# A recommendation tower on one core: ten of the first block's 32 table gathers replaced by comparisons and TensorE products, and the split of the second filter cut into pieces

## The reference, cut to what matters

```python
e = jnp.stack([tbl_f[ids[:, f]] for f in range(32)], axis=1)     # (512, 32, 32), all fp32
for W in (filter_0, filter_1):                                   # (1024, 128), (4096, 128)
    z = jnp.einsum('bhd,bmd->bhmd', e, prev)                     # prev: e, then the first layer
    cur = relu(jnp.einsum('bpd,pn->bnd', z.reshape(b, h * m, d), W)); prev = cur
h = concatenate([sum over d of both layers, dense_ctx], axis=1)  # (512, 272)
y = relu(relu(h @ W_top1 + b1) @ W_top2 + b2) @ W_top3
```

## Time and profile before

| | |
|---|---|
| median of 3 runs | 885.71 us (884.96 to 886.36) |
| profiled execution | 882.99 us |
| its span (first to last instruction) | 881.2 us |
| around the span | 1.8 us |
| PE matmul / DVE / ACT / POOL busy | 94% / 88% / 82% / 75% |

### The profile page before, as it was taken

The page is one execution under the profiler, slowest core; times in us unless marked ns, Lnnn a source line. Parts: engine busy times, 40 slices in busy tenths (PEclk is TensorE's granted clock), DMA queues, the critical chain, the costliest instruction groups (busy, mean ns, idle before and its releaser), DMA issues.

```text
span 881.2 us, 18094 instructions
## 1 busy us (share of the span) xinstructions
PE 832.6 (94%) x3608; PEld 669.4 (76%) x3608; DVE 771.7 (88%) x2425; ACT 724.7 (82%) x2425; POOL 662.0 (75%) x645
## 2 busy tenths in 40 slices
PE   0189999999999999999999999999999999999998
PEld 0068888888887788887888878888888888888875
DVE  4248999999998999998999999999999999999995
ACT  2248889988888899888888988888889988888883
POOL 7777898878887888868888878876677766666662
PEclk9999999999999999999999999999999999999999
DMA  7035776667667666666677666766776667657540
GB/s 197 12 88 129 176 170 148 134 127 172 153 152 168 156 151 142 127 158 154 155 174 166 145 135 130 169 145 151 171 168 141 133 135 158 153 138 171 96 93 5
DMA packets 78622, 124.42 MB, mean 141 GB/s; under 512 B 34177, under 2 KB 36993, under 8 KB 78594
## 3 DMA queue, kind: packets, MB, share of 16 engines
q0 software_dynamic: 22240, 68.17, 40.9%
q1 hardware_dynamic: 56354, 55.96, 21.0%
HBM read 54.99 MB, written 3.05 MB: 66 GB/s over the span
## 4 chain that ended last, share of the span: by engine, by line
PE 80%; POOL 9%; issue 5%; DVE 3%; DMA 2%; ACT 0%; POOLq 0%; DVEq 0%; ACTq 0%
PE bank L879 68%; PE bank L819 10%; POOL rows L349 4%; DVE acc L780 2%; POOL pair_low L384 2%; DMA parts<-parts 1%; POOL w_sb L368 1%; POOL rows_next L399 1%; PE bank L885 1%; POOL parts L361 1%; PE bank L911 1%; PE bank L850 1%; DVE acc L790 0%; POOL half L368 0%; DMA rows<-table_dram,ids_sb 0%
## 5 line engine op out<-in xcount | busy, mean ns | idle before, releaser
L560 ACT ACTIVATE parts<-bank,x 128x128 f32<-128x128 f32 x2048 | 588.0, 379 | 98.3 <-PE bank L879 87.2
L780 DVE SCALAR_TENSOR_TENSOR acc<-bank,x,acc 128x128 f32<-128x128 f32 x1792 | 484.2, 341 | 44.6 <-PE bank L879 44.6
L879 PE MATMUL bank<-w_high,cur_high 128*128 128x512 f32 x1024 | 402.3, 393 | 0.8 <-ACT cur_high L507 0.7
L879 PE MATMUL bank<-w_low,cur_high 128*128 128x512 f32 x1024 | 399.5, 390 | 0.0
L879 PE MATMUL bank<-w_high,cur_low 128*128 128x512 f32 x992 | 388.3, 391 | 0.0
L879 PEld LDWEIGHTS bank<-w_high,cur_high 128*128 128x128 f32 x1024 | 192.3, 188 | 48.2 <-DVE acc L780 6.4
L879 PEld LDWEIGHTS bank<-w_low,cur_high 128*128 128x128 f32 x1024 | 192.4, 188 | 40.0
L879 PEld LDWEIGHTS bank<-w_high,cur_low 128*128 128x128 f32 x992 | 186.2, 188 | 40.6
L384 POOL TENSOR_TENSOR pair_low<-pair,pair_high 128x512 fp32r<-128x512 f32 x124 | 158.8, 1300 | 22.0 <-ACT pair_high L496 19.2
L368 POOL TENSOR_TENSOR half<-parts 128x512 f32<-128x512 f32 x64 | 82.8, 1293 | 120.0 <-DMA parts<-parts 119.9
L399 POOL DMA_INDIRECT rows_next<-table_dram,ids_next x96 | 97.9, 1019 | 30.6 <-issue 30.3
(11 more groups left out here) (96 smaller groups left out, 557.9 us busy)
## 6 DMA issues: line engine op xcount, KB each, us to landing
parts<-parts POOLq DMA_DIRECT2D x126, 512.0 KB, 6.7
shifts<-x_scratch SPq DMA_DIRECT2D x155, 256.0 KB, 3.9
x<-x_scratch SPq DMA_DIRECT2D x31, 256.0 KB, 2.9
x_scratch<-turned SPq DMA_DIRECT2D x124, 24.0 KB
rows_next<-table_dram,ids_next POOLq DMA_INDIRECT x96, 5.0
wt<-w_top_dram SPq DMA_DIRECT2D x2, 512.0 KB, 9.1
rows<-table_dram,ids_sb POOLq DMA_INDIRECT x32, 2.4
w_sb<-w_ab_dram SPq DMA_DIRECT2D x1, 256.0 KB, 3.0
```

What stands on the lines that cost most here:

```text
L560: ins = nc.scalar.activation(parts[q][ab][:, at:at + N2], act_bank[ab][:, i * N2:(i + 1) * N2], ACT.Copy, scale=x0[u][:, h, 2 * q + ab:2 * ...
L780: nc.vector.scalar_tensor_tensor(out=dst, in0=dve_bank[e % 2 * 2 + ab][:, i * N2:(i + 1) * N2], scalar=x0[u][:, h, 2 * q + ab:2 * q + ab + ...
L879: return nc.tensor.matmul(dst[:], cur_half[u][:, cols], w1_half[:, fields], **flags)
```

## The change

The ten tables 9, 12, 22, 25 to 31 that are small (eight of 1000 rows, two of 1250) are loaded whole for block 0: row p * k + r of a table goes to partition p of 125, at place r of k (k = 8 or 10). Their 1280 ids are loaded to all 128 partitions and put into three PSUM banks as fp32. For each of the k places DVE compares the ids of a set of tables (four, four, two) with `p * k + r`, which gives a matrix of zeros and ones, table rows by samples; PE multiplies it by the table's rows, adding over the places: 4 x 8 + 4 x 8 + 2 x 10 = 84 products with 128 stationary and 32 moving columns, all fp32, into one PSUM bank. ACT copies that bank into `rows` in four pieces. The other 22 tables are gathered as before. Blocks 1 to 3 are not touched.

The second filter is split in eight pieces of 512 columns on ACT and DVE, behind the comparisons on DVE and behind the dense input on ACT. SP issues the new loads early (ids before the first filter, tables behind it) and the dense pieces ahead of the second filter. PE's 16 products without a reader stand behind the 84, and wait for one piece of `w1_high` and the first 16 gathers. `dve_turn` moves behind the three spreads.

```diff
+SMALL = {9: 8, 12: 8, 22: 8, 26: 8, 27: 8, 28: 8, 30: 8, 31: 8, 25: 10, 29: 10}
+SMALL_SETS = [(9, 12, 22, 26), (27, 28, 30, 31), (25, 29)]
+ROW_COPIES = [(9, 10), (12, 13), (22, 23), (25, 32)]
+GATHERED = [f for f in range(F) if f not in SMALL]
+LAST_FIELDS = (18, 25)
+FIRST_COPIES = 4
+W1_PIECES = 8
...
             sp.dma_start(ids_sb[:], ids.rearrange("(k p) f -> p k f", p=P)).then_inc(ids_in, 16)
+            sp.dma_start(ids_wide, bass.AP(small_ids.tensor, small_ids.offset,
+                                              [[0, P], [1, len(SMALL) * P]])).then_inc(small_ids_in, 16)
+            sp.dma_start(first_row[:], small_rows).then_inc(small_ids_in, 16)
...
+            for i, fields in enumerate(SMALL_SETS):
+                for f in fields:
+                    sp.dma_start(small_tables[f][0:SMALL_ROWS, :],
+                                 tables[f].rearrange("(p k) d -> p (k d)", k=SMALL[f])).then_inc(small_in[i], 16)
+            for row in range(0, P, F):
+                sp.dma_start(dense_raw[0][row:row + DENSE, :], w_top1[2 * P:, :]).then_inc(dense_in, 16)
+                sp.dma_start(dense_raw[1][row:row + DENSE, :], dense_t).then_inc(dense_in, 16)
             sp.dma_start(w1_sb[:], w1.rearrange("(h m) n -> m h n", h=F)).then_inc(w1_in, 16)
...
-            for f in range(F):
+            for f in sorted(GATHERED, key=lambda f: LAST_FIELDS[0] <= f < LAST_FIELDS[1]):
...
-            pool.wait_ge(first_gathered[0], (F - LAST_TABLES) * 16)
+            pool.wait_ge(first_gathered[0], (len(GATHERED) - LAST_TABLES) * 16)
             pool.wait_ge(first_gathered[1], LAST_TABLES * 16)
+            pool.wait_ge(small_copied, len(ROW_COPIES))
...
+            act.wait_ge(w1_in, 16)
+            for piece in range(W1_PIECES):
+                nc.scalar.copy(w1_high[:, piece * 512:(piece + 1) * 512],
+                               w1_flat[:, piece * 512:(piece + 1) * 512]).then_inc(w1_high_done, 1)
+            act.wait_ge(small_picked, len(SMALL))
+            for first_field, end_field in ROW_COPIES:
+                at = slice(AT[first_field] * D, (AT[end_field - 1] + 1) * D)
+                nc.scalar.copy(rows[:, 0, first_field:end_field, :].rearrange("p f d -> p (f d)"),
+                               small_bank[:, at]).then_inc(small_copied, 1)
+            act.wait_ge(first_fields_ready, FIRST_COPIES)
+            act_spread(2)
+            act.wait_ge(small_copied, len(ROW_COPIES))
             act_turn_waits(act, 1)
             act_turn(act, 1)
-            act.wait_ge(first_fields_ready, 3)
-            act_spread(2)
...
+            nc.vector.memset(wt1_dense[:].bitcast(FP32), 0.0).then_inc(dense_zeroed, 1)
+            nc.vector.memset(dense_sb[:].bitcast(FP32), 0.0).then_inc(dense_zeroed, 1)
+            dve.wait_ge(small_ids_in, 2 * 16)
+            for i, fields in enumerate(SMALL_SETS):
+                width = len(fields) * P
+                nc.vector.tensor_copy(small_ids_bank[i][:, 0:width],
+                                      ids_wide[:, i * 4 * P:i * 4 * P + width]).then_inc(small_ids_copied, 1)
...
+            for i, fields in enumerate(SMALL_SETS):
+                width = len(fields) * P
+                dve.wait_ge(small_ids_copied, i + 1)
+                for r in range(SMALL[fields[0]]):
+                    nc.vector.tensor_scalar(one_hot[i][r], small_ids_bank[i][:, 0:width], first_row[:, i // 2, r:r + 1],
+                                            None, ALU.is_equal).then_inc(one_hot_done, 1)
+            for piece in range(W1_PIECES):
+                dve.wait_ge(w1_high_done, piece + 1)
+                at = slice(piece * 512, (piece + 1) * 512)
+                nc.vector.tensor_tensor(w1_low[:, at], w1_flat[:, at], w1_high[:, at].bitcast(FP32),
+                                        ALU.subtract).then_inc(w1_low_done, 1)
...
+            dve.wait_ge(small_copied, len(ROW_COPIES))
+            dve.wait_ge(first_gathered[0], (len(GATHERED) - LAST_TABLES) * 16)
+            first_copy(0, 0, LAST_FIELDS[0])
             first_copy(F, 0, SHIFTS)
+            first_copy(LAST_FIELDS[1], LAST_FIELDS[1], F)
             dve.wait_ge(first_gathered[1], LAST_TABLES * 16)
-            first_copy(F - LAST_TABLES, F - LAST_TABLES, F)
-            dve_turn(dve, 1)
-            dve.wait_ge(first_fields_ready, 3)
+            first_copy(LAST_FIELDS[0], *LAST_FIELDS)
+            dve.wait_ge(first_fields_ready, FIRST_COPIES)
             for step in (-1, 1, 0):
                 nc.vector.tensor_copy(spread_out(step), first_fields(step)).then_inc(dve_wide, 1)
+            dve_turn(dve, 1)
...
             pe.wait_ge(w0_done, 4)
-            pe.wait_ge(w1_low_done, 1)
-
-            pe.wait_ge(first_gathered[0], (F - LAST_TABLES) * 16)
+            one_hots = 0
+            for i, fields in enumerate(SMALL_SETS):
+                count = SMALL[fields[0]]
+                one_hots += count
+                pe.wait_ge(one_hot_done, one_hots)
+                pe.wait_ge(small_in[i], len(fields) * 16)
+                for j, f in enumerate(fields):
+                    for r in range(count):
+                        ins = nc.tensor.matmul(small_bank[:, AT[f] * D:(AT[f] + 1) * D],
+                                               one_hot[i][r][0:SMALL_ROWS, j * P:(j + 1) * P],
+                                               small_tables[f][0:SMALL_ROWS, r * D:(r + 1) * D],
+                                               start=r == 0, stop=r == count - 1)
+                    ins.then_inc(small_picked, 1)
+            pe.wait_ge(w1_high_done, 1)
+            pe.wait_ge(first_gathered[0], (len(GATHERED) - LAST_TABLES) * 16)
             keep_busy(WARM_UP, warm_bank)
...
             for step in FIRST_ORDER:
                 pe_product(pe, 0, step, FIRST_ORDER)
+            pe.wait_ge(w1_low_done, W1_PIECES)
```

More of the change, by code:

```diff
@@ L71 @@
 LAST_TABLES = 6
+SMALL = {9: 8, 12: 8, 22: 8, 26: 8, 27: 8, 28: 8, 30: 8, 31: 8, 25: 10, 29: 10}
+SMALL_SETS = [(9, 12, 22, 26), (27, 28, 30, 31), (25, 29)]
+SMALL_ROWS = 125
+AT = {f: i for i, f in enumerate(sorted(SMALL))}
+ROW_COPIES = [(9, 10), (12, 13), (22, 23), (25, 32)]
[3 more added lines that the diff above has]
+W1_PIECES = 8
 WARM_UP = 16
 def dlrm_tower(nc, ids, tables, w0_ab, w0_ba, w0_half, w1, w_top1, b_top1, w_top2, b_top2, w_top3, dense_t,
-               identity, parity, x0_dram, out):
+               identity, parity, small_ids,
+               small_rows, x0_dram, out):
     ctx = ExitStack()
@@ L87, in dlrm_tower @@
         ids_sb = sb("ids_sb", [P, BLOCKS, F], INT32)
+        first_row = sb("first_row", [P, 2, max(SMALL.values())])
         ids_next = sb("ids_next", [P, F], INT32)
@@ L129, in dlrm_tower @@
         z1 = x4[0]
+        w1_flat = w1_sb[:].rearrange("p h n -> p (h n)")
         free = w1_sb[:].rearrange("p h n -> p (h n)")
@@ L150, in dlrm_tower @@
         first_wide = [parts[1][i // 4][:, i % 4 * COLS:(i % 4 + 1) * COLS] for i in range(1 + STEPS)]
+        ids_wide = parts[0][0][:, 768:768 + len(SMALL) * P].bitcast(INT32)
+        small_tables = {}
+        for f in SMALL:
+            at = sum(SMALL[g] * D for g in SMALL if SMALL[g] == SMALL[f] and g < f)
+            small_tables[f] = parts[1][SMALL[f] == 10][:, at:at + SMALL[f] * D]
+        spare_tiles = [shifts[u][:, step, :] for u in range(2) for step in range(STEPS)] + [r[:] for r in raw]
+        spare_tiles += [rows[:, block_no, i * (F // 2):(i + 1) * (F // 2), :].rearrange("p f d -> p (f d)")
+                        for block_no in range(1, BLOCKS) for i in range(2)] + [half_a[:, 0, :]]
+        one_hot = [spare_tiles[0:8], spare_tiles[8:16],
+                   [spare_tiles[16 + i // 2][:, i % 2 * 256:(i % 2 + 1) * 256] for i in range(10)]]
         def first_fields(step):
@@ L166, in dlrm_tower @@
         z2_bank = cur_bank
-        first_bank, warm_bank = [bank[5]] + dve_bank + [bank[4]], bank[7]
+        first_bank, warm_bank = [bank[5]] + dve_bank + [bank[4]], cur_bank
+        small_ids_bank, small_bank = bank[0:3], bank[7]
         def pair16_bank(chunk):
@@ L184, in dlrm_tower @@
         w1_in = sem("w1_in")
+        small_ids_in = sem("small_ids_in")
+        small_in = [sem(f"small_in_{i}") for i in range(len(SMALL_SETS))]
+        small_ids_copied = sem("small_ids_copied")
+        one_hot_done = sem("one_hot_done")
+        small_picked = sem("small_picked")
+        small_copied = sem("small_copied")
         w0_in = sem("w0_in")
@@ L305, in _ @@
             sp.dma_start(bt2[:], b_top2).then_inc(top_in, 16)
-            for row in range(0, P, F):
-                sp.dma_start(dense_raw[0][row:row + DENSE, :], w_top1[2 * P:, :]).then_inc(dense_in, 16)
-                sp.dma_start(dense_raw[1][row:row + DENSE, :], dense_t).then_inc(dense_in, 16)
             def shift_through_dram(c, u):
@@ L351, in _ @@
                     in_offset=bass.IndirectOffsetOnAxis(ids_sb[:, 0, f:f + 1], 0)).then_inc(
-                        first_gathered[f >= F - LAST_TABLES], 16)
```

(31 more changed lines are left out.)

## The result

| | before | after |
|---|---|---|
| median | 885.34 us | 947.84 us (946.99 to 948.57, 4 runs) |
| ratio after to before, 95% interval | | 1.0705 (1.0684 to 1.0725) |
| profiled execution, and its span | 882.99, 881.2 | 948.57, 946.7 |
| first product of the loop | 59.13 | 66.16 |
| from there to the end of the span | 822.1 | 880.5 |

The start came out as forecast: the loop begins 7.0 us later (6.9 forecast). The other 58.4 us are in the loop, where I had forecast nothing.

The account below looks back on a forecast made before the run. PE bounds the kernel (80% of the chain). Start: 15.8 + 0.3 + 36.3 for the passes, 6.4 for 16 products, 7.2 to the loop at 66.0 against 59.13; 885.71 + 6.9 = 892.6 us, range 873.5 to 896.5.

Parts of the forecast that it names:

- The step that failed: Loop: it runs at PE's pace and the change touches nothing in it, so only the start moves, by +6.9 us.
- the range: Whole kernel: the forecast time lies between 873.5 and 896.5 us.
- The gathers: POOL, start: 21 steps of 1.245 us remain, last gather issued at 29.8 and landed at 32.2 us.
- The split: Second filter in pieces, start: POOL finds gaps between them, so the stall of 3.86 us goes, with 0.3 left.
- The comparisons: DVE, start: 26 comparisons from about 11.0 us, 0.60 or 0.38 each, sets ready at 15.8, 20.6 and 24.4.
- the 16 products: PE, behind the 84: products without a reader start when the 84 are done and take 6.4 us, to 58.8.
- The pass: PE, 84 products: 168 passes at the low clock, 0.216 us each, 36.3 in all; chance 0.54.
- the clock rises under the 84 products: Rival, PE: low clock for 5.6 us only, loop starts 10.5 us earlier, 875.2 us; chance 0.26.
- The rival of the unslowed load: PE: the load doesn't slow with the clock, passes of 0.112, loop 10.6 us earlier, 875.1 us; chance 0.07.
- Behind them: PE, after the 84 and 16 products: transposes, first filter and rounding take 7.2 us; loop starts at 66.0.
- The transposes: PE, before the loop: no idle time ahead, so they find the high clock and take 2.6 us instead of 4.43.
- the second filter: Load, start: it lands near 22 us, not late for what follows.

Follow-up runs that it names:

- e1: The kernel before plus 37 DVE writes of one column to a tile of their own, ahead of the loop: 940.61 us, ratio 1.062.
- e4: The kernel before with only the second filter's split in eight pieces, plus 121 DVE writes (loop at 342): 881.67 us, ratio 0.9951.
- e5: The changed kernel with its DVE loop at 342, plus five fp32 products of 512 columns ahead of the 84: 887.26 us, ratio 1.0016.
- e2: The changed kernel plus 91 DVE writes ahead of the loop, which then starts at instruction 342: 890.54 us, ratio 1.005.
- e7: The changed kernel with four tables picked instead of ten, plus 111 DVE writes (loop at 342): 874.69 us, ratio 0.9871.

## Why the prediction was wrong, step by step

**The step that failed** is the first one: "So the loop runs at PE's pace, and the change touches nothing in it: whatever it does must show in the start", with its conclusion, "everything behind follows it". The change edits no line of the loop, but it moves the loop's place in DVE's program by 37 instructions. That cost 58.4 us in the changed kernel's loop, and e1 shows it alone at 54.6 in the medians. No rival had it, so the range missed by 51 us. The profile before had what was needed to ask: a queue that fetches instructions, on the page that I had read, and 13 short waits for "issue" at the body's top (2.5 us in all), as many as the jumps back, in the list of waits, which I had read for the first 66 us only. I gave neither a price.

**The start was right, and most of its terms were; two errors in it cancelled.**
- The gathers: forecast last issue 29.8, measured 30.27. No gather was longer than 1.36 us. The split frees POOL, as e4 shows alone: its last gather is issued 3.7 us earlier, against the 3.56 of the forecast (3.86 less 0.3).
- The comparisons: first one forecast at 11.0, measured 11.60; third set ready at 24.4, measured 26.1. PE began at 17.2, not at 16.1 (15.8 and 0.3 for the first product): the comparisons began 0.6 us later, and eight of them took 5.28 us, 0.66 each and not 0.60. This 1.1 us was made good by the 16 products (5.55 instead of 6.4) and by the passes (0.3). That the sum came out within 0.2 us is in part luck.
- The pass: 0.216 forecast, 0.2144 measured, for all 168. The record of the granted clock of the changed kernel begins at 56.95 only, behind them; that it is the low level follows from e5, where a pass took the same 0.2144 at a granted clock of 0.50. The rival "the clock rises under the 84 products" is refuted more firmly than I had put it, 0.54 to 0.26: e5 gave it the high clock to begin with, and it was lost. The rival of the unslowed load is refuted too: the load's rule of the Trainium skill (TensorE: Matmul & The Clock Gate, "LDWEIGHTS"), 107 ns for 128 columns, is half of what a pass takes at 1.2 GHz; at 2.4 GHz e5 has 0.112, as I had taken it.
- Behind them: loop at 66.0 forecast, 66.16 measured. The transposes found the high clock, 2.80 us. The reason that I gave, that no idle time is left ahead of them, is not borne out: in e1 and e4 they found it too, after 3.15 and 2.98 us of idle time.
- Where I was too early was the second filter: forecast to land near 22, it came at 30.5, since SP needed 8.45 us to issue the ten tables, its load was issued at 17.55 only, and it took 13.0 us to land instead of 10.4. DVE hid it, as it idled until 53.97 anyway.

**The whole without the displaced loop** is e2: 890.54 us. That is 4.5 us above the kernel before in the medians (3.1 to 5.7 by the interval) and 7.2 in the spans of the two profiled executions. In the traces the loop begins 7.1 us later (66.27 against 59.13), so the mechanism and the sign of my 6.9 hold; the timed size is smaller, and its interval leaves 6.9 out. Part of this lies in the execution on which I had built: at 882.99 us it was 3.1 under the median of 886.06, while that of e2 was 0.3 under its own. Where in the span the other executions of the kernel before spend those 3 us no trace shows. It is not the clock of the transposes: e1, whose start is that of the kernel before, had them in 3.02 us and its loop at 57.49, 1.6 earlier than 59.13, and that would make the difference larger. Behind the start the seven kernels without stalls took 821.3 to 824.0 us to the end of the span, so a spread of this size is there too.

**What stays open.** Which places are good beyond 86 and bad beyond 123 and 15. "A body that lies in three pieces of 128 stays, one in four does not" does not fit the counts as they stand: from 86 a body of 327 reaches into a fourth piece, and from 15 it does not. It fits all the kernels only if each program has 63 to 99 more instructions ahead of the ones counted (or 128 more than that, and so on), and I did not count those. Nor did I look for the edges, or for why the stall at 271 is shorter (2.8 us). Nor did I try whether the loops of the other engines, whose bodies are shorter, would stall at some place.

## What to carry to other kernels

A hardware loop's place in its engine's program can be part of its performance, as it was for this one: after any edit ahead of a loop, look at the wait for "issue" in front of the body's first operation and at the packets of the instruction queue, and if they have grown, put idle instructions in front until the place is that of before, or shorten the body. When work is moved from a slow engine to an idle one, move only so much that both end together: five tables of ten gained 14 us where ten lost 5 (e2). Passes with few moving columns should be costed from rows at the low clock, loads included: here one of 32 columns took 0.2144 us at 1.2 GHz and 0.112 at 2.4.

## What the runs showed of the hardware that I had not expected

- A jump back over a DVE body of 327 instructions cost 0.2 us at the places 214 and 342, and 2.8 to 3.4 us at 251, 271 and 379. In the changed kernel the first fetch went 0.16 us after the stall began.
- DVE's stall of 3.45 us took PE's clock with it: PE idled 3.04 us, the granted clock fell, and its next products followed each other in 0.43 us for some 3.5 us.
- TensorE's clock fell to 1.2 GHz under 168 weight loads and products without a gap, after it had been at 2.4 GHz at their start (e5), and did not rise in 28 us of them.
- The clock was not always lost with idle time: PE idled 3.15 us in e1 and 2.98 in e4, and the transposes behind found 2.4 GHz; after 2.34 us in e7 and 2.48 in the kernel before they found 1.2.
